# Graph network on one core: turning a group's strips by the identity and adding its tiles one by one

## The reference

```
h   = segment_sum(x[src], dst) + x
h1  = batchnorm(h @ W1 + b1)                  # 256 -> 1024, over the nodes
x   = layernorm(x + relu(relu(h1) @ W2 + b2)) # 1024 -> 256
# three times, l = 1..3, with deg counted over dst (and one more loop per node):
h   = relu(segment_sum((h @ Wl.T)[src] * dinv[src] * dinv[dst], dst) + bl)
x   = layernorm(x + h)
```

## Time and profile before

| what | value |
| --- | --- |
| median of three runs | 2980.72 us |
| the profiled execution: time, and span from first to last instruction | 2979.73 us, 2977.9 us |
| busy: TensorE, VectorE, ScalarE, GpSimd | 2430.8, 1436.1, 956.7, 2028.7 us |
| pass 0, matrix layer, pass 1, pass 2, pass 3 end at about | 1130, 1349, 1880, 2420, 2978 us |
| VectorE busy in passes 1, 2 and 3 | 148.5, 148.2 and 171.4 us |

### The profile page before, as it was taken

How to read it: one execution, slowest core, us unless ns; L and a number is a source line. 1 busy time by engine, 2 the same in 40 slices (tenths; PEclk the granted TensorE clock), 3 DMA queues, 4 the chain that set the end, 5 groups by cost and what they waited for, 6 DMA issues and landing times.

```text
span 2977.9 us, 45883 instructions
## 1 busy us (share of the span) xinstructions
PE 2430.8 (82%) x15812; PEld 1798.0 (60%) x15812; DVE 1436.1 (48%) x3530; ACT 956.7 (32%) x1512; POOL 2028.7 (68%) x2155
## 2 busy tenths in 40 slices
PE   3667676667666768989999987899999888999986
PEld 2445454444444447777777765677777566777764
DVE  7777777777778766661323233122222321324234
ACT  0111111111111115544444443344444344343431
POOL 6677777777777750017777776677777757777773
PEclk9987778878878788999999999899999999999997
DMA  4454444455444437987888898779898977888793
GB/s 136 133 162 142 159 152 150 159 160 162 143 159 158 141 130 256 334 282 251 298 287 288 290 325 285 239 258 309 265 315 295 332 238 260 272 271 272 258 329 103
DMA packets 361538, 681.84 MB, mean 229 GB/s; under 512 B 44243, under 2 KB 190633, under 8 KB 355403
## 3 DMA queue, kind: packets, MB, share of 16 engines
q0 software_dynamic: 103152, 296.88, 31.5%
q10 hardware_dynamic: 154688, 222.02, 22.4%
q1 hardware_dynamic: 103451, 159.81, 15.4%
HBM read 560.99 MB, written 117.51 MB: 228 GB/s over the span
## 4 chain that ended last, share of the span: by engine, by line
PE 59%; DVE 19%; DMA 8%; issue 6%; DVEq 3%; ACT 2%; POOL 0%; SPq 0%; ACTq 0%
PE ps L1048 29%; PE ps L915 8%; DVE vreg L1229 7%; PE ps L953 7%; PE ps L897 5%; DMA hbuf<-parts_d 4%; PE ps L963 4%; PE ps L1032 3%; PE ps L927 1%; DVEq L1222 1%; DMA xs<-x_d 1%; DVE vreg L1209 1%; DVE vreg L1210 1%; DVE vreg L1216 1%; DMA xs<-in_x_dram 1%
## 5 line engine op out<-in xcount | busy, mean ns | idle before, releaser
L613 POOL DMA_INDIRECT ring<-table_d,idx x1248 | 1192.1, 955 | 452.2 <-issue 377.8
L1048 PE MATMUL ps<-wide,hbuf 128*128 128x512 f32 x4116 | 1048.3, 407 | 44.7 <-DMA hbuf<-parts_d 33.4
L613 POOL DMA_INDIRECT ring<-in_x_dram,idx x832 | 820.9, 987 | 269.2 <-issue 251.6
L1048 PEld LDWEIGHTS ps<-wide,hbuf 128*128 128x128 f32 x4116 | 767.5, 193 | 271.4 <-issue 63.5
L771 ACT CAST wide<-abuf 128x1024 fp32r<-128x1024 uint8 (+1 forms) x588 | 552.5, 940 | 646.2 <-PE ps L1048 643.9
L1189 DVE TENSOR_TENSOR acc<-acc,ps 128x256 f32 x260 | 107.7, 414 | 672.1 <-PE ps L915 667.4
L927 PE MATMUL ps<-vreg 128*128 128x300 bf16 x832 | 206.3, 361 | 269.2 <-DVE vreg L1229 225.2
L915 PE MATMUL ps<-place,strips 128*128 128x128 f32 x2080 | 328.8, 309 | 64.4 <-ACT strips L660 34.1
L1229 DVE TENSOR_TENSOR vreg<-vreg,ps 128x600 f32 x416 | 328.3, 789 | 96.4 <-DVE vreg L1229 55.5
L915 PEld LDWEIGHTS ps<-place,strips 128*128 128x128 f32 x2080 | 306.0, 219 | 104.5 <-ACT strips L660 53.2
L897 PE MATMUL ps<-ring,hot 128*32 128x256 f32 x4160 | 323.3, 432 | 50.9 <-issue 32.6
(11 more groups left out here) (127 smaller groups left out, 1533.9 us busy)
## 6 DMA issues: line engine op xcount, KB each, us to landing
hbuf<-parts_d ACTq DMA_DIRECT2D x84, 1024.0 KB
hbuf<-parts_d ACTq DMA_DIRECT2D x84, 768.0 KB
abuf<-ad_d ACTq DMA_DIRECT2D x63, 896.0 KB, 8.0
parts_d<-vreg SPq DMA_DIRECT2D x72, 512.0 KB, 4.9
h_d<-ureg SPq DMA_DIRECT2D x23, 1024.0 KB, 7.5
ureg<-h_d POOLq DMA_DIRECT2D x23, 1024.0 KB, 8.2
ad_d<-vreg SPq DMA_DIRECT2D x28, 784.0 KB, 4.3
ring<-table_d,idx POOLq DMA_INDIRECT x1248
```

The lines of the kernel that those rows point to most:

```text
L613: pool.indirect_dma_start(out=ring[:, i % SLOTS, j, :], out_offset=None, in_=table[0:N, :], in_offset=at).then_inc(g["rows"][i % SLOTS], 16)
L1048: ins = pe.matmul(ps[:, 2 + 4 * q + h, 0:(n1 - 4 * q) * P].rearrange("p (s n) -> p s n", n=P), hbuf[:, bl, e * D + h * P:e * D + (h + 1) * P],
```

## The change

In passes 1 to 3 the placing one-hot is no longer written. The strips of a group are turned by four transposes against the identity (`turn_strips` in place of `group_sums`) and stay in the order of the tiles. VectorE then makes eight adds, one for each tile, of 32 columns in two halves each, at the column where this tile begins (`add_strips` in place of `add_group`). It reads eight starts into registers for it; each add waits until the one before it is counted, and the counts of `acc` go in eights. The tiles' starts are made once, in group 1 of pass 0: TensorE brings the tiles' smallest destinations into one row (`sparse_rows`) and VectorE writes them as bounded integers to `tilec` (`tile_starts`). Pass 0 works as before.

```diff
+            def sparse_rows():
+
+                pe.wait_ge(s_kt, 2)
+                at = 0
+                for g0, g1 in GATHERED:
+                    for j in range(TILES):
+                        ins = pe.matmul(ps[0:1, 0, at:at + g1 - g0], gcol[:, 2 + j:3 + j], ident[0:NG, g0:g1],
+                                        start=True, stop=True)
+                        at += g1 - g0
+                ins.then_inc(s_kt, 1)
+
+            def turn_strips(a, i):
+                g = aggs[a]
+                pe.wait_ge(g["kept"], i + 1)
+                wait(pe, g["acc"], i * TILES)
+                for at in range(0, HALVES * D, P):
+                    ins = pe.transpose(ps[:, 5, at:at + P], strips[:, i % 2, at:at + P], ident[:, :])
+                ins.then_inc(g["sum"], 1)
...
@@ TensorE, pass 0 and passes 1-3
+                if k == 1:
+                    sparse_rows()
...
-                    group_sums(a, i)
+                    turn_strips(a, i)
...
+            def tile_starts():
+
+                dve.wait_ge(s_kt, 3)
+                at = 0
+                for g0, g1 in GATHERED:
+                    n, i = (g1 - g0) * TILES, SPARSE.index(g0) * TILES
+                    dve.tensor_scalar(tilec[:, i:i + n].rearrange("p (g j) -> p j g", j=TILES),
+                                      ps[0:1, 0, at:at + n].rearrange("p (j g) -> p j g", g=g1 - g0),
+                                      0.0, float(NCOL - NARROW), ALU.max, ALU.min)
+                    at += n
+                dve.drain()
...
@@ make_hot
+                ins = dve.tensor_tensor(hot[:, i % 2, :, :], rel[:, k, :].unsqueeze(2).to_broadcast([P, TILES, NARROW]),
+                                        iota[:, 0:NARROW].unsqueeze(1).to_broadcast([P, TILES, NARROW]), ALU.is_equal)
+                if a > 0:
+                    ins.then_inc(g["hot"], 1)
+                    return
...
+            def add_strips(a, i):
+
+                g = aggs[a]
+                starts = [dve.value_load(tilec[0:1, n:n + 1], min_val=0, max_val=NCOL - NARROW)
+                          for n in range(i * TILES, (i + 1) * TILES)]
+                dve.wait_ge(g["sum"], i + 1)
+                turned = ps[:, 5, :].rearrange("p (u h j n) -> p u h j n", u=HALVES, h=DH, j=STRIPS)
+                for j, start in enumerate(starts):
+                    wait(dve, g["acc"], i * TILES + j)
+                    to = acc[:, :, bass.ds(start, NARROW)]
+                    dve.tensor_tensor(to, to, turned[:, j // STRIPS, :, j % STRIPS, :], ALU.add).then_inc(g["acc"], 1)
...
@@ VectorE, passes 1-3
-                    add_group(a, i, k)
+                    add_strips(a, i)
                     for n, c in enumerate(AT1[i]):
-                        take(a, s, r + n, c, ((aggs[a]["acc"], i + 1), (s_dacc, done)))
+                        take(a, s, r + n, c, ((aggs[a]["acc"], (i + 1) * TILES), (s_dacc, done)))
...
-                        dve.wait_ge(aggs[a]["acc"], i + 1)
+                        dve.wait_ge(aggs[a]["acc"], (i + 1) * TILES)
```

More of the change, by code:

```diff
@@ L72, in gnn_kernel @@
     NSP = len(SPARSE)
+    GATHERED = [(e0, e1) for e0, e1 in zip([0] + [g1 for _, g1 in DENSE], [g0 for g0, _ in DENSE] + [NG]) if e0 < e1]
     EVERY = list(range(NG))
@@ L189, in gnn_kernel @@
         ctl = sb("ctl", [1, NG], I32)
+        tilec = sb("tilec", [1, NSP * TILES], I32)
         offs = sb("offs", [1, NT], I32)
@@ L916, in group_sums @@
                                         place[:, i % 2, u, :], start=(u == 0), stop=(u == HALVES - 1))
[L917 to L920, removed]
+                for u in range(HALVES):
+                    ins = pe.matmul(ps[0:1, 5, DH * WIN:DH * WIN + WIN], counts[:, i % 2, u:u + 1],
+                                    placeb[:, i % 2, u, :], start=(u == 0), stop=(u == HALVES - 1))
                 ins.then_inc(g["sum"], 1)
@@ L1193, in make_hot @@
                 wait(dve, g["sum"], i - 1)
-                dve.tensor_tensor(hot[:, i % 2, :, :], rel[:, k, :].unsqueeze(2).to_broadcast([P, TILES, NARROW]),
-                                  iota[:, 0:NARROW].unsqueeze(1).to_broadcast([P, TILES, NARROW]), ALU.is_equal)
+                ins = dve.tensor_tensor(hot[:, i % 2, :, :], rel[:, k, :].unsqueeze(2).to_broadcast([P, TILES, NARROW]),
[3 more added lines that the diff above has]
+                    return
                 dve.tensor_tensor(place[:, i % 2, :, :], shift[:, k, :].unsqueeze(2).to_broadcast([P, HALVES, WIN]),
@@ L1368, in _ @@
                     tile_rows(step)
+                if k == 1:
+                    tile_starts()
                 if AT0[k]:
```

## The result

The changed kernel takes 3353.44 us (median of four runs, 3346.39 to 3354.88) against 2981.94 us (2976.0 to 2983.96) for the kernel before on the same chip: a ratio of 1.1244, 95% interval 1.1211 to 1.1277. The profiled execution took 3352.58 us, span 3350.7, that is 372.9 us more than the one of before. The forecast was 255 us more; the direction came as forecast, the size lay 118 us above it and 33 us above the range.

What follows compares the result with a forecast made beforehand. The gather and TensorE's order paced passes 1-3, with VectorE's loop to set the new rounds. Passes 75 + 75 + 88, clock 15 and pass 0 2 made 255 us on 2979.73: 3235 us, range 3115 to 3320.

Steps and rivals of the forecast that it cites:

- dense runs: Consecutive chunk groups 10-14, 24-29, 38-42: rounds of 13.74 us, adding 12.4, 16.4 and 3.5 us in pass 1.
- between them: Stretches between runs of chunk groups in pass 1: +5.4, -5, +3.5 and +5.2 us.
- closing groups: Groups 45-51: +17.4, +9.4 and +6.6 us in pass 1, plus 15 for the lower clock in passes 1 and 2.
- pass 0, and from pass to pass: Pass 0, group 1: 32 small matmuls and four 1-partition operations that VectorE waits for, at most 4.8 us, taken as 2.
- The size of an add: VectorE, each of a group's eight adds: 0.22 us for 64 columns, extended from adds of 256 and 512 columns.
- the length of pass 3's `rows_done`: Pass 3: 4.1 us to the next `make_hot` for 3.1, no longer hidden, so 13 dense rounds gain 1.0 each.
- The distance of the adds: VectorE: each add waits for the one before, 0.35 us apart, so eight take 2.65 us for 0.42.
- The dense runs keep 70% busy; I leave them.: TensorE in the dense runs: no lower clock priced there, only 15 us in the closings of passes 1 and 2.
- rival 4: Clock falls in the dense runs too: 13 rounds x 3 x 1.5 us on `layer`, +60, total 3295; chance 18%.
- 5.05 us for the loads: VectorE behind `rows_done`: eight register loads up to the first add, uncovered, 5.05 us each time, 5.9 at the longest.
- 19.1 us: Dense stage's end, last group's add to next `layer`: 2.45 + 5.05 + 2.96 + 5.05 + 2.65 + 0.94, along VectorE.
- Its clock term: Closing groups of passes 1 and 2: TensorE at its lower clock, 5 rounds x 1.5 x 2 = +15 us.

Runs made afterwards that it cites:

- run 9: Changed kernel with last dense step's matmuls repeated in chunk groups following a chunk group, and row stores held until next group's adds in passes 1 and 2: 3270.68 us.
- Run 3: Changed kernel with one register load and one add per group, seven of each left out: 2972.83 us, against 2977.47 for the kernel before.
- run 7: Changed kernel with a group's eight starts read by one load instruction into eight registers, bounds checks kept: 3119.04 us.
- run 8: Changed kernel with the next group's eight loads moved right behind `take`, ahead of the dense adds and `rows_done`: 3121.02 us.
- run 10: Changed kernel with one load instruction for a group's eight starts, placed right behind `take`; the eight adds stay: 3043.67 us.
- run 1: Changed kernel with one register load per group, all eight adds going to the first tile's column: 3016.73 us.
- run 5: Changed kernel with the last dense step's matmuls repeated only in chunk groups that follow a chunk group: 3310.47 us.
- run 6: Changed kernel with SyncE's row stores in passes 1 and 2 held until the next group's adds are done: 3315.63 us.

## Why the prediction was right in its direction and wrong in its size

From `layer` to `layer`, added time by kind of stretch, us, all three passes (the forecast's terms, the changed kernel's profile, and run 9's):

| stretch | forecast | changed kernel | run 9 |
| --- | --- | --- | --- |
| dense runs (10-14, 24-29, 38-42) | 3 x 32.3 + 13 = 109.9 | 64.0 + 61.0 + 55.5 = 180.5 | 36.3 + 35.0 + 38.7 = 110.0 |
| between them (7-10, 14-24, 29-38, 42-45) | 3 x 9.1 = 27.3 | 23.4 + 21.7 + 21.4 = 66.5 | 19.0 + 23.4 + 18.9 = 61.4 |
| closing groups (45-51) | 3 x 33.4 + 15 = 115.2 | 47.6 + 45.4 + 36.9 = 129.9 | 44.0 + 42.2 + 38.1 = 124.2 |
| pass 0, and from pass to pass | 2 | -4.1 | -7.2 |

**Right.** The mechanism: register loads behind the last awaited step of `rows_done`, covered by nothing, and adds that wait for each other. Run 3 shows that without both the change costs nothing, and runs 7, 8 and 10 that it is the loads' number and place in VectorE's queue which count. The size of an add (0.222 us, forecast 0.22), the turn (0.60 us), the placing one-hot (nothing), the gather's pace, the length of pass 3's `rows_done`. The distance of the adds is right too (0.354 us, forecast 0.35), but not all for the reason given: in run 1, where each still waits for the one before, it is 0.257, so 0.10 of the gap of 0.13 goes with the register instruction ahead of each add. The earlier trace rows had such a pair as well, so the number held. The Trainium skill's "Perfetto Trace Analysis" (section "Optimizing Scalar/DVE Operations") has half of an instruction's latency overlap with the next; for adds that each wait for the one before the trace of the changed kernel shows the opposite, 0.13 us between the end of one and the start of the next, as the earlier trace rows did; in run 1 it is still 0.03.

**Wrong, first: "The dense runs keep 70% busy; I leave them."** The share came out right (74%), the conclusion did not. What `layer` met was not the mean over the round but the stand of 3.3 to 6.7 us just ahead of it, and it ran at the lower of the two clock levels, wholly or in part, on the very path that sets the round: 36 of the 39 `layer` in these rounds took 2.4 us or more, 52 us together above 1.99 each. I had the rows to see it: in pass 3's closings a `layer` at 3.78 us. That was rival 4, with 18% and +60; run 5 recovers 43 us, though its filling doesn't bring back every `layer`.

**Wrong, second: 5.05 us for the loads.** The earlier trace rows had the right eight loads, but at a place where no rows were being stored. Behind a chunk the same loads meet the store of that chunk's rows; from `make_hot` to the first add they took 5.9 us in the round shown. I kept 5.9 as an end of the range, from the longest row, without asking what made it longest. The loads of the dense rounds take 31 us more than 0.30 each (14.5, 13.1 and 3.3 in the three passes), and run 6 gives 38 us for two passes. With both causes taken away, run 9, the dense runs cost 110.0 us for 109.9 forecast.

That this agrees to a tenth is in part luck. It is 36.3 and 35.0 us against 32.3 in passes 1 and 2, and 38.7 against 45.3 in pass 3: there I added 13 us for the longer `rows_done` to pass 1's sum, though pass 3's dense runs were already 11.8 us longer before the change (158.2 us for 146.4). So the two causes make 52 + 31 us and this error takes 12 back, which is the 71 us that the changed kernel's dense runs lie above the forecast. The 5.05 itself is idle time behind the end of an instruction, and I counted it from the start of `make_hot` and left out the 0.43 us of that; in run 9 the idle time is 4.64 and `make_hot` 0.47, so the sum came out right by chance.

**Wrong, third: the stretches between, 27 us forecast and 67 measured.** Run 9 leaves 61 of them, so neither clock nor stores in the dense runs explain them. The timelines give the reasons, read from the trace of the changed kernel and not tested by a run of their own. At a stage's end I followed VectorE alone from the last group's add to the next `layer` (19.1 us). VectorE after group 21 to 24 of pass 1:

```profile
1612.52 2.70 DVE L1254 TENSOR_TENSOR acc<-acc,ps 128x64 f32 x8 [4.61 <-issue]
1620.12 2.96 DVE L1480 TENSOR_TENSOR acc<-acc,ps 128x256 f32 x8 [4.89 <-issue]
```

and TensorE there:

```profile
1623.22 10.30 PE L1071 MATMUL ps<-wide,hbuf 128*128 128x512 f32 x32 [6.83 <-DVE acc L1480]
1633.36 1.89 PE L984 MATMUL ps<-wt_s,us 128*128 128x256 f32 x8
```

The next stage's dense steps wait for the dense adds, and 10.1 us of them stand ahead of `layer`, so it is TensorE that ends last: 1633.36 - 1612.52 = 20.8 us. It is the clock again, which I had priced for the closing groups alone: behind the stand of 6.83 us these 32 matmuls take 10.30 us, at a granted clock of 0.71. The same 32 after group 9 of the kernel before took 7.50, at 1.00:

```profile
1448.55 7.50 PE L1048 MATMUL ps<-wide,hbuf 128*128 128x512 f32 x32
```

At that pace, by an estimate from these rows, VectorE would have ended last, at 19.7 us. With 1.3 us more from group 21 up to there, 1.1 of it loads beside a store, that makes 39.8 us from 21 to 24 where I had 36.75. Groups 7 to 10 go the same way: 20.0 us to group 9's add where I had 17.65, and 20.9 from there where I had 19.1. From 14 to 21 I had 59.2 us, and it took 62.3: the first late add costs TensorE a wait of 2.24 us ahead of group 16's turn (I had 1.4), and the dense matmuls that follow it take 7.35 us for 24, at a granted clock of 0.77, where the same 24 take 5.7 at the next groups. How much of the 40 us each of these makes over all passes stays open.

In the closing groups the forecast held within 15 us. Its clock term (1.5 us a round) was a little low, as `layer` goes from 1.99 to 3.78, and the loads there meet stores too (run 9's 124.2 for 129.9 is what the later stores give back).

## What to carry to other kernels

Count what stands in an engine's queue behind its last awaited step: register loads there cost their whole time, however little they depend on, and both fewer instructions (one load for eight registers) and an earlier place (behind the last thing that others wait for) take much of it away (runs 7, 8 and 10). When a change makes TensorE wait inside a round, price the work behind the wait at the lower clock as well, from rows of the same instruction after a stand, and not by the busy share of the stretch. And look for the bound on both sides of each wait: a stretch followed along one engine is only a lower bound.

## What the runs showed of the hardware that was not expected

- A register load of VectorE takes 0.30 us alone and 0.65 to 0.75 beside the row stores on SyncE's queue (means by place in the row; 0.30 again with the stores moved away). One instruction that loads eight registers takes 0.60 us, 0.81 beside the stores.
- Adds whose addresses come from eight registers stand 0.354 us apart, with a register instruction of 0.05 us ahead of each; with one register for all, and the same waits, 0.257 (run 1).
- Matmuls repeated to no use made the kernel faster by some 40 us (runs 5 and 9). The stand ahead of `layer` tells only in part which clock it meets. In the changed kernel `layer` of a full chunk took 1.99 us or less in the 20 cases with a stand under 3 us or none, and 3.4 to 3.8 in the 29 with 4 us or more. In run 5 stands of 1.98 and 2.05 us were followed by 3.16 and 2.97 us, and one of 2.90 by 1.99.
